# A neighbour gather in two row tiles, and the last residual adds of a sweep layer moved to VectorE

## The reference

```python
counts = 1 + round(normalised |laplacian of the channel mean| * 7)      # per pixel
sim    = cosine similarity of each pixel with its 3x3 neighbours        # 9 per pixel
wts    = exp(sim), kept for the `counts` most similar, normalised to sum 1
out    = sum over the 9 neighbours of wts * neighbour                   # all 128 channels
enhanced = out + group_norm(x)
h   = relu(w1 @ enhanced + b1)                                          # 128 -> 256
return enhanced + w2 @ h + b2                                           # 256 -> 128
```

## Time and profile before

| | us |
|---|---|
| median of 3 runs (range) | 6434.84 (6428.44 to 6439.73) |
| the profiled execution, its own time | 6428.9 |
| span of the profiled execution | 6426.9 |
| TensorE matmul busy | 5265.2 (82%) |
| VectorE busy | 4264.0 (66%) |
| GpSimd busy | 2582.3 (40%) |
| ScalarE busy | 2377.9 (37%) |
| mean granted TensorE clock | 0.909 of full speed |

### The profile page before, as it was taken

One profiled execution on the slowest core, in us unless ns is written; L12 is line 12 of the kernel. 1 busy time (PEld: TensorE's weight loads), 2 busy tenths in 40 slices (PEclk: granted clock), 3 DMA queues, 4 the chain that ended last, 5 costly groups with the idle time before them and its releaser, 6 DMA issues. The chain is left out here.

```text
span 6426.9 us, 129253 instructions
## 1 busy us (share of the span) xinstructions
PE 5265.2 (82%) x49774; PEld 4307.3 (67%) x49774; DVE 4264.0 (66%) x7220; ACT 2377.9 (37%) x4272; POOL 2582.3 (40%) x1460
## 2 busy tenths in 40 slices
PE   2878787878787877156859587999979999999997
PEld 1656565656555555044647465777779999999997
DVE  5767677777676767567768658999833333455565
ACT  1666666656565665122323126665510000000000
POOL 1535454445354544245747457888800000000021
PEclk9989898888898988588979798999989999999998
DMA  3000000000000000222223110110140000000034
GB/s 134 15 28 15 28 28 15 28 28 17 27 21 22 27 17 16 85 69 67 91 71 100 40 63 15 50 47 37 36 150 0 0 0 0 0 0 0 0 52 131
DMA packets 215659, 252.28 MB, mean 39 GB/s; under 512 B 157216, under 2 KB 158496, under 8 KB 208032
## 3 DMA queue, kind: packets, MB, share of 16 engines
q1 hardware_dynamic: 83872, 229.30, 10.2%
q10 hardware_dynamic: 131328, 16.78, 1.7%
HBM read 139.49 MB, written 67.11 MB: 32 GB/s over the span
## 5 line engine op out<-in xcount | busy, mean ns | idle before, releaser
L2332 DVE SCALAR_TENSOR_TENSOR l_state<-l_conv,l_state 128x256 f32 x500 | 292.4, 585 | 794.7 <-PE l_conv L2257 794.7
L527 POOL TENSOR_TENSOR l_probs<-l_probs,l_inv 128x1024 f32<-128x1024 f32 x256 | 493.0, 1931 | 567.9 <-DVE l_inv L937 567.3
L1438 PE MATMUL l_gather_ps<-l_wdiag,l_stage 128*128 128x128 f32 x4608 | 546.9, 279 | 163.9 <-DVE l_wdiag L1593 163.8
L1438 PEld LDWEIGHTS l_gather_ps<-l_wdiag,l_stage 128*128 128x128 f32 x4608 | 536.9, 195 | 208.0 <-issue 150.1
L2257 PE MATMUL l_conv<-l_carry_hi,l_taps_hi 128*128 128x248 f32 (+2 forms) x4500 | 628.5, 284 | 38.3 <-DVE l_carry_hi L2317 38.3
L2296 POOL TENSOR_TENSOR l_state<-l_state,l_xres 128x2048 f32<-128x2048 f32 x8 | 37.1, 4670 | 1475.7 <-DVE l_carry_lo L2319 1475.7
L2257 PE MATMUL l_conv<-l_carry_lo,l_taps_hi 128*128 128x248 f32 (+2 forms) x4500 | 622.8, 283 | 7.4 <-DVE l_carry_lo L2319 7.4
L2257 PE MATMUL l_conv<-l_carry_hi,l_taps_lo 128*128 128x248 f32 (+2 forms) x4500 | 627.7, 285 | 0.0
L2257 PEld LDWEIGHTS l_conv<-l_carry_hi,l_taps_hi 128*128 128x128 f32 x4500 | 580.4, 191 | 41.8 <-DVE l_carry_hi L2317 41.7
L2109 DVE SCALAR_TENSOR_TENSOR l_acc<-l_xpad,l_w,l_acc 128x1024 f32<-128x1024 f32 x448 | 574.5, 1289 | 14.8 <-ACT l_acc L2010 1.3
L1929 POOL TENSOR_TENSOR l_sum<-l_sum,l_prod 128x1024 f32<-128x1024 f32 x224 | 538.9, 2406 | 111.0 <-ACT l_prod L2026 92.3
(11 more groups left out here) (293 smaller groups left out, 9856.7 us busy)
## 6 DMA issues: line engine op xcount, KB each, us to landing
l_xleft<-l_xt SPq DMA_DIRECT2D x64, 283.5 KB
l_xright<-l_xt SPq DMA_DIRECT2D x64, 283.5 KB
stat_xs<-in_x SPq DMA_DIRECT2D x8, 2048.0 KB, 23.1
l_hats<-in_x SPq DMA_DIRECT2D x8, 2048.0 KB, 7.7
l_xraw<-in_x SPq DMA_DIRECT2D x8, 2048.0 KB, 8.6
after_layer<-l_xraw SPq DMA_DIRECT2D x64, 256.0 KB, 2.0
l_xblk<-after_layer SPq DMA_DIRECT2D x32, 512.0 KB, 4.6
l_xres<-after_layer SPq DMA_DIRECT2D x32, 512.0 KB, 4.4
```

What stands on the lines that cost most here:

```text
L527: pool.tensor_tensor(part, part, inv[:, u, cols].rearrange("c (j o) -> c j o", o=1).to_broadcast([C, 4, KEYS]), ALU.mult).then_inc(scaled_ ...
L1438: last = pe.matmul(gather_ps[u][y // 4][:, y % 4 * C:(y % 4 + 1) * C], stage[:, u, y + k // 3, :], wdiag[:, y % SLOTS, k, :], start=(k == ...
L2332: dve.scalar_tensor_tensor(row, conv[h][:, 0:HB * W].rearrange("c (b w) -> c b w", b=HB), 0.0, row, op0=ALU.max, op1=ALU.add).then_inc(lin ...
```

## The change

In layer 1 the gather is organised by source row. A step of 8 target rows has 10 source rows. For each source row `s`, each horizontal offset `dx` and each image `b`, one matmul takes the 64 partitions of that image (a row tile of TensorE) and up to 3 x 64 = 192 columns, the target rows that the source row feeds. It accumulates onto one bank per image. The set of matrices of one source row has 3 x 3 x 64 = 576 elements per partition (192 for `s` = 0 and 9, 384 for 1 and 8), in 10 slots. GpSimd makes the sets 4 and 7, VectorE the other eight. The group norm's product is now made by TensorE: two more matmuls, `affine`, at the start of its step, with `xres` as an operand; its addend comes in at the copy out of PSUM, `enhance`, now on ScalarE. ScalarE also copies the stage. After each `weights`, three copies and one more lay out the weights by source row. In layer 3 VectorE does all adds of the left half, those of the first 4 images between its last sweep steps.

```diff
-    BY_DVE, BY_POOL = (0, 2, 3, 5, 6), (1, 4, 7)
+    SOURCES = ROWS + 2
+    BY_DVE, BY_POOL = (0, 1, 2, 3, 5, 6, 8, 9), (4, 7)
...
+            def build(t, c, s):
+
                 g = (t - 1) * STEPS + c
                 pool.wait_ge(weights_shifted, WS * t)
...
+                wait(pool, row_done, (g - 1) * SOURCES + (s + 1))
+                apart(pool, c)
+                pool.tensor_tensor(wdiag[:, s, :, :, :],
...
                     if t >= 1:
-                        build(t, c, 1)
+                        build(t, c, 4)
                     if second_before(t, c):
                         result(c + ((t - 1) * STEPS - 2), u, 0)
                     if t >= 1:
-                        build(t, c, 4)
+                        build(t, c, 7)
                     if second_before(t, c):
                         result(c + ((t - 1) * STEPS - 2), u, 1)
...
-                    if t >= 1:
-                        build(t, c, 7)
...
+            def affine(t, c, u):
+
+                g = (t - 1) * STEPS + c
+                pe.wait_ge(res_loaded[u], (g + (2 - u)) * 8)
+                if isinstance(c, int) and c == 0:
+                    pe.wait_ge(gdiag_ready, t)
+
+                wait(pe, enh_ready, (g - 1) * 2)
+                for b in range(2):
+                    pe.matmul(gather_ps[u][b][:, :], gdiag[:, b, :], xres[:, u, b, :], start=True, stop=False)
+
+            def gather(t, c, u, *sources):
+                g = (t - 1) * STEPS + c
+                for s in sources:
...
+                    first, final = targets(s)
+                    for dx in range(3):
+                        for b in range(2):
+                            at = slice(64 * b, 64 * b + 64)
+                            last = pe.matmul(gather_ps[u][b][:, (s - 2 + first) * W:(s - 1 + final) * W], stage[at, u, s, :],
+                                             wdiag[at, s, dx, first:final + 1, :].rearrange("p j x -> p (j x)"), start=False,
+                                             stop=(s == SOURCES - 1 and dx == 2))
                     last.then_inc(row_done, 1)
...
                     if t >= 1:
-                        gather(t, c, u, (0, 1))
+                        affine(t, c, u)
+                        gather(t, c, u, 0, 1)
                     if before:
                         hidden(g, 1 - u, 0)
                     if t < PAIRS:
                         turn(t, c, u)
                     if t >= 1:
-                        gather(t, c, u, (2, 3))
+                        gather(t, c, u, 2, 3, 4)
                     if before:
                         down(g, 0)
                         hidden(g, 1 - u, 1)
                     if t >= 1:
-                        gather(t, c, u, (4, 5))
+                        gather(t, c, u, 5, 6)
                     if before:
                         down(g, 1)
                     if t >= 1:
-                        gather(t, c, u, (6, 7))
+                        gather(t, c, u, 7, 8, 9)
...
+            def enhance(t, c, u):
+
+                g = (t - 1) * STEPS + c
+                act.wait_ge(row_done, (g + 1) * SOURCES)
...
+                    if t >= 1:
+                        put_stage(t, c, u)
+                    if before:
+                        enhance(*block_before(t, c, 1), 1 - u)
                     if t < PAIRS:
                         norm(t, c, u)
...
+                for e in range(3):
+                    last = dve.tensor_copy(wout[:, 2 - e, :, e:e + H], sim[:, 3 * e:3 * e + 3, :])
+                link(last)
+                dve.tensor_copy(wsrc[:, :, 1, :], wout[:, :, 1, :]).then_inc(weights_ready, 1)
...
             for steps, parts in stretches():
+                if parts[0] == (1, 3, STEPS[3] - LEAD) and len(parts) == 1:
+                    dve.wait_ge(lo_ready[0], BEFORE[3] + STEPS[3] + 1)
+                    for q in range(LEAD):
+                        step(1, 3, STEPS[3] - LEAD + q)
+                        if q < HB:
+                            add_left(2 * q, 2 * q + 1)
+                    continue
```

More of the change, by code:

```diff
@@ L1194, in layer1 @@
         turn_ps = [mem.psum("turn_ps")]
-        gather_ps = [[mem.psum(f"gather_ps{u}{half}") for half in range(2)] for u in range(2)]
+        gather_ps = [[mem.psum(f"gather_ps{u}{b}") for b in range(2)] for u in range(2)]
         hid_ps = [mem.psum(f"hid_ps{h}") for h in range(2)]
@@ L1425, in turn @@
                     last.then_inc(turned, 1)
-            def gather(t, c, u, rows):
+            def affine(t, c, u):
                 g = (t - 1) * STEPS + c
-                for y in rows:
-                    if y == 0:
-                        pe.wait_ge(staged, g + 1)
[L1433 to L1439, removed]
+                pe.wait_ge(res_loaded[u], (g + (2 - u)) * 8)
[7 more added lines that the diff above has]
+                for s in sources:
+                    if s == 0:
+                        pe.wait_ge(staged, g + 1)
+                    if s in BY_DVE:
+                        pe.wait_ge(diag_dve, g * len(BY_DVE) + (BY_DVE.index(s) + 1))
+                    else:
+                        pe.wait_ge(diag_pool, g * len(BY_POOL) + (BY_POOL.index(s) + 1))
+                    first, final = targets(s)
[5 more added lines that the diff above has]
+                                             stop=(s == SOURCES - 1 and dx == 2))
                     last.then_inc(row_done, 1)
             def hidden(g, u, b):
-                pe.wait_ge(enh_ready, g * 2 + 2)
+                pe.wait_ge(enh_ready, g * 2 + (b + 1))
                 for h in range(2):
@@ L1586, in _, with build, scales @@
             link = chain.link
-            def build(t, c, *rows):
+            def build(t, c, *sources):
                 g = (t - 1) * STEPS + c
[L1590 to L1611, removed]
+                for s in sources:
+                    first, final = targets(s)
+                    n = final + 1 - first
+                    wait(dve, row_done, (g - 1) * SOURCES + (s + 1))
+                    dve.tensor_tensor(wdiag[:, s, :, first:final + 1, :],
+                                      diag[:, :, :].rearrange("p d (o x) -> p d o x", o=1).to_broadcast([C, 3, n, W]),
+                                      wsrc[:, first:final + 1, :, bass.ds(c * ROWS + s, 1)].rearrange("p j d o -> p d j o")
+                                      .to_broadcast([C, 3, n, W]), ALU.mult).then_inc(diag_dve, 1)
+            def scales(t):
+                wait(dve, row_done, (t - 1) * STEPS * SOURCES)
+                for b in range(2):
+                    n = 2 * (t - 1) + b
+                    last = dve.tensor_scalar(gdiag[:, b, :], sh.ident[:, :], gscale[:, n:n + 1], None, ALU.mult)
+                last.then_inc(gdiag_ready, 1)
             def stats(t, c, u):
@@ L1731, in _ @@
                     dve.wait_ge(weights_shifted, WS * t)
+                if t >= 1:
+                    scales(t)
                 def step(c, u):
-                    before = t >= 1 and not (isinstance(c, int) and t == 1 and c == 0)
-                    g = (t - 1) * STEPS - 1 + c
+                    lagging = t < PAIRS and not (isinstance(c, int) and c == 0)
                     if t >= 1:
[L1737 to L1741, removed]
+                        build(t, c, 0, 1, 2)
                     if lagging:
```

88 lines of the change are left out of this document (39 added, 49 removed).

## The result

| | before | after |
|---|---|---|
| median of 4 runs, us (range) | 6433.57 (6428.44 to 6439.73) | 6578.19 (6576.47 to 6581.87) |
| ratio, 95% interval | | 1.0225 (1.0207 to 1.0243) |
| span of the profiled execution | 6426.9 | 6577.0 |
| mean granted TensorE clock | 0.909 | 0.886 |

The kernel became slower by 2.25%, 144.6 us; the forecast was 6549, some 114 us slower. The first part of the page alone would mislead: TensorE, VectorE and GpSimd are each busy for fewer microseconds than before, and the span is 150.1 us longer.

A forecast was written before the change was run, and what follows sets the result against it. No single bound over the span; in layer 1 TensorE never idles in pass 4 and is busy 24.56 of 27.41 us before it. 6428.9 + 116 - 2 = 6542.9, with 5.9 for the median 6549 us; range 6450 to 6650.

The forecast's parts named there:

- The loop over `affine`, source row 7, `build` 7, `result` image 1 and the load: Layer 1, from one step's `affine` to the next: sets the step, 27.8 us in pass 4, 30.1 in passes 1 to 3.
- TensorE, `affine` until GpSimd starts `build` 7: Layer 1 step, pass 4: TensorE's work through source row 7, 16.4 us at full clock, plus 2.5 for half clock.
- GpSimd, `build` 7 and `result` image 1: Layer 1 step, pass 4: one 576-element set, 1.1 us, then two additions, 3.0 us, before the load can go out.
- load and wake: Layer 1 step: the residual load takes 4.4 us, bounds 3.6 and 5.4, and waking 0.1.
- The restart at half clock: Layer 1, each step: after its idle TensorE restarts at half clock, 2.5 us more, bounds 2.0 and 2.7.
- The sum for layer 1: All of layer 1: start of pass 1, step intervals, last step and pass entries together cost +116 us.
- The three entries: Layer 1, entries to passes 2, 3 and 4: TensorE starts later by 9.2 us each, +28 in all.
- Layer 3: Left-half adds moved to VectorE: sweep may end up to 9 us sooner, the end hardly moves, -2, bounds -9 and +3.
- the load is there in time: Rival, layer 1: `affine` does not wait, the kernel gets faster by about 170 us, to 6265; chance 0.11.
- the row tiles take turns: Rival, layer 1 gather: the two images' matmuls do not run together, 8.0 us more a step, 6740 us; chance 0.07.
- the clock holds: Rival, layer 1: TensorE keeps full clock despite its idle, 2.5 us less in 27 steps, 6481 us; chance 0.10.
- rival 3: Layer 1: the rival that TensorE's clock holds despite the idle, 6481 us; chance 0.10.

The follow-up runs named there:

- experiment 1: Changed kernel, but `affine` reads its own copy of the residual block by its own load, with four weight tiles laid over product tiles: 6336.1 us, ratio 0.9856.
- experiment 3: Changed kernel with one swap in GpSimd's order, `result` image 1 ahead of `build` 7: 6490.61 us, ratio 1.0096.
- experiment 2: Kernel before the change with only the layer 3 part of the change, VectorE making all left-half adds: 6433.7 us, ratio 1.0003.
- experiment 5: Kernel of experiment 1 with `affine`'s loads issued earlier, scale matrices made earlier, and layer 3 as before the change: 6313.51 us, ratio 0.9814.
- experiment 4: Changed kernel with six more 512-column matmuls, read by nobody, at the end of each gathered step: 6500.91 us, ratio 1.0112.

## Why the prediction was right, and where its numbers were off

**The mechanism.** The loop over `affine`, source row 7, `build` 7, `result` image 1 and the load is there in the order forecast. TensorE waits for the load 5.4 to 7.9 us in a step, inside or just under the 6 to 10 expected. Taking the load off the loop (experiment 1) removed 242 us, and shortening it at one place (experiment 3) 88 us.

**The terms of the loop**, forecast and then measured in the step of pass 4 above:

| term | forecast | measured |
|---|---|---|
| TensorE, `affine` until GpSimd starts `build` 7 | 16.4 + 2.5 | 3869.42 - 3847.26 = 22.16 |
| GpSimd, `build` 7 and `result` image 1 | 1.1 + 3.0 | 3872.20 + 1.26 - 3869.42 = 4.04 |
| SyncE's issue | 0.25 | 3873.71 - 3873.46 = 0.25 |
| load and wake | 4.4 + 0.1 | 3877.98 - 3873.71 = 4.27 |
| step | 27.8 | 30.72 |

Three of the four stood. The step that failed is the size of TensorE's term, and in it two parts:

- *The restart at half clock*, taken as 2.5 us from the earlier trace rows. Here `affine` to source row 2 takes 3857.08 - 3847.26 = 9.82 us. The same instructions without a wait before them take 5.37 in experiment 1 (timeline, 3613.73 - 3608.36):

```profile
3608.36 1.98 PE L1452 MATMUL l_gather_ps<-l_xaff,l_gdiag 128*128 128x512 f32 x4
3610.28 1.61 PE L1467 MATMUL l_gather_ps<-l_wdiag,l_stage 64*128 64x64 f32 x24
3611.82 1.98 PE L1477 MATMUL l_hid_ps<-l_enh,l_w1T 128*128 128x512 f32 x4
3613.73 3.20 PE L1467 MATMUL l_gather_ps<-l_wdiag,l_stage 64*128 64x192 f32 x36
3616.86 1.98 PE L1483 MATMUL l_ffn_ps<-l_hid,l_w2T 128*128 128x512 f32 x4
...
3626.07 1.17 POOL L1379 TENSOR_TENSOR l_wdiag<-l_diag,l_wsrc 128x576 f32<-128x576 f32 x1 [3.68 <-PE l_gather_ps L1467]
```

  So the restart cost 4.45 us in this step, outside the forecast's bounds, and as much in five others of pass 4's eight (9.79 to 9.95 us for the stretch; the first two took 7.24 and 6.93). The bounds, 2.0 and 2.7, came from two restarts after one long idle each, and the forecast took them for the size of any restart.
- *TensorE's own work* until GpSimd starts `build` 7, at full clock: 3626.07 - 3608.36 = 17.7 us in experiment 1 against 16.4. Source rows 0 and 1 took 1.54 us (3611.82 - 3610.28) where columns gave 0.35 + 0.67 = 1.02, and a full row 1.04 to 1.08 instead of 0.99, so the short matmuls of these rows do not go by columns alone. From the end of row 7 to GpSimd's start it is 1.52 - 1.04 = 0.5 us where 0.16 was taken. The groups of 512 columns, `affine` among them, fit: 1.91 or 1.92 us beside a change of tile in these rows, where 1.72 and 0.1 for each change were taken. (The forecast's 8.20/72 is 0.114, not 0.112; that moves nothing here.)

The Trainium skill, TensorEngine Tiling (Array Packing), Key Properties, says that a change of tiling mode drains TensorE. These rows agree with a small price: 1.92 - 1.72 = 0.2 for `affine`, which has a change on both sides, so the 0.1 each that was taken.

In passes 1 to 3 the size came out nearly right, 30.3 to 30.6 us on average against 30.1, and that was luck: two errors met. The chain of a step of pass 2, one of the shorter (timeline of the changed kernel):

```profile
3278.82 3.78 PE L1441 MATMUL l_gather_ps<-l_xres,l_gdiag 128*128 128x512 f32 x4 [5.72 <-DMA l_xres<-after_layer]
3282.52 1.87 PE L1456 MATMUL l_gather_ps<-l_wdiag,l_stage 64*128 64x64 f32 x24
...
3300.54 1.25 POOL L1369 TENSOR_TENSOR l_wdiag<-l_diag,l_wsrc 128x576 f32<-128x576 f32 x1 [3.67 <-PE l_gather_ps L1456]
...
3304.92 0.37 SPq L1303 DMA_DIRECT2D l_xres<-after_layer  x1
3308.45 1.22 PE L1441 MATMUL l_gather_ps<-l_xres,l_gdiag 128*128 128x512 f32 x1 [5.50 <-DMA l_xres<-after_layer]
```

TensorE's part is 3300.54 - 3278.82 = 21.72 us where 20.8 was forecast, GpSimd's and SyncE's together 4.38 where it was 4.75, and the load 3.53 where it was 4.5. The median load from issue to landing was 3.6 us in these passes and 4.2 in pass 4; the earlier trace rows had given 4.4 for both. An error of +0.9 met one of -1.3. This step takes 29.63 us; behind the first, the steps of passes 2 and 3 take 29.6 to 30.1 or 31.8 to 32.2, and the restart goes with them: `affine` to source row 2 takes 9.3 to 9.8 us in the former and 11.5 to 11.7 in the latter, against 7.33 in experiment 1. So the restart costs 2 to 4.4 us there, too, and in the longer steps it outweighs the load's gain.

**The sum for layer 1**, +116 forecast and +145.5 measured. Passes 1 to 3: +54 forecast, +62 measured. Pass 4: +34 forecast, +47 measured (29.95 on average against 27.8); the restart weighs most there, where the change had most to lose. The three entries: +28 forecast; from the start of a pass's last step to the start of the next pass's first, 91.3 us became 103.4 on average, +36 in all. The entry to pass 4:

```profile
3716.42 1.17 POOL L1369 TENSOR_TENSOR l_wdiag<-l_diag,l_wsrc 128x576 f32<-128x576 f32 x1 [61.98 <-DMA l_wsrc<-l_wout]
...
3729.75 3.78 PE L1441 MATMUL l_gather_ps<-l_xres,l_gdiag 128*128 128x512 f32 x4 [41.96 <-DMA l_xres<-after_layer]
```

From GpSimd's first set to `affine` that is 13.3 us, and 12.6 and 12.4 at the other two, where the forecast had 12.3 and the kernel before 4.1: this part was right. The rest arises ahead of it. From the start of a pass's last step to GpSimd's first set it was 87.2 us before, 88.1 in experiment 1 (entry to pass 3) and 90.6 after. The first 0.9 is the layout, forecast as 1; the other 2.5 come with the half clock in the last step, which the forecast left out. The start of pass 1 (-1 for +3) and the last step (0 for -3) were small.

**Layer 3**, -2 forecast. In the two traces it is 4.6 us longer (1735.0 and 1739.6), outside the bound of +3; experiment 2, over many runs, shows no difference within 0.12%, some 8 us. Single traces scatter by as much: with the old adds it is 1740.2 us in experiment 5, with the new ones 1737.3 in experiment 1 and 1741.0 in experiment 2. So that step was right in kind, and its size is below what these runs tell.

**The rivals.** (The range 6450 to 6650 left out the 0.04 for no change, too, so 0.22 in all and not 0.18.) That the load is there in time fell at once: the wait is there 32 times. That the row tiles take turns fell with the 1.04 us of a full row. That the clock holds fell with the 0.50 in the window above, and experiment 4 shows what holding it would have been worth in the changed kernel: at least 77 us. Behind the idle that rival 3 asked about, here 5.4 to 7.9 us, the granted clock was 0.50 over the first 2 us of all 28 steps; behind one of 2.0 to 2.4 us, in pass 4 of experiment 4, it fell in some steps and not in others.

What stays open is what sets the size of a restart. In pass 2 of the changed kernel `affine` to `turn` takes 5.27 us at full clock (3191.28 to 3196.55 in experiment 1); it took 7.47 us after an idle of 7.79 and, a step later, 9.49 after one of 6.33. The length of the idle before it does not order them, and no run held it constant.

## What to carry to other kernels

When an operation moves to the front of an in-order engine, ask first when each operand's buffer is released and by whom: a double buffer whose last reader runs two steps later closes a loop through every queue between, and where that loop is longer than each engine's own work, it is the step. Add to such a loop the half clock behind an idle of TensorE: here each idle of 5 us or more was paid twice. And when a cheaper operation makes the kernel slower, look for the new wait before taking the edit back: with a buffer of its own the same gather made the kernel 1.4% faster than before the change, and 1.9% with the loads issued earlier.

## What the runs showed of the hardware that was not expected

- Six useless matmuls a step, 12 instructions of 512 columns that take 5.42 us at full clock (timeline of experiment 4), made the changed kernel 77 us faster: the mean granted clock rose from 0.886 to 0.908.
- Two row tiles of 64 partitions overlap nearly as well when three matmuls of one are issued before three of the other (1.18 us a source row) as when they alternate (1.04), against an estimated 1.98 in turn.
- After an idle of 7.69 us TensorE ran at a granted clock of 0.50 still 5.7 to 7.7 us into its work, with TensorE busy all the time.
